# A two-block layer kernel on one core: the first W2 turned by VectorE instead of TensorE, and the attention constants made two row groups later

## The reference

```python
xn = _layernorm(x)
s = _L0_attn_ref(xn, ...)                        # state starts at zero: xn + rmsnorm(xn @ M) for one matrix M
g = _silu(_L0_ffn_ref(xn, W1, W2, W3))
x = x + s * g
...
# a feed-forward part, the same in both blocks
hidden = jax.nn.silu(xn @ W1.T) * (xn @ W3.T)    # 1024 wide
hidden = fwht(hidden)                            # Walsh-Hadamard transform over the 1024
out = hidden @ W2.T
...
# attention of block 1 (causal, one head, 256 wide)
q, k, v = x_norm @ qkv[:, :K], x_norm @ qkv[:, K:2*K], x_norm @ qkv[:, 2*K:]
out = softmax(mask(q @ k.T / 16)) @ v @ o_proj + residual
```

## Time and profile before

| | |
|---|---|
| time, median of 3 runs | 355.83 us (355.63 to 355.95) |
| the profiled execution's own time | 355.57 us |
| its span on the core | 353.8 us |
| TensorE busy | 348.7 us, 99% |
| VectorE busy | 252.5 us, 71% |
| ScalarE busy | 168.3 us, 48% |
| GpSimd busy | 106.3 us, 30% |

### The profile page before, as it was taken

One profiled execution on the slowest core, in us unless ns is written; L12 is line 12 of the kernel. 1 busy time (PEld: TensorE's weight loads), 2 busy tenths in 40 slices (PEclk: granted clock), 3 DMA queues, 4 the chain that ended last, 5 costly groups with the idle time before them and its releaser, 6 DMA issues.

```text
span 353.8 us, 4943 instructions
## 1 busy us (share of the span) xinstructions
PE 348.7 (99%) x1761; PEld 295.9 (84%) x1761; DVE 252.5 (71%) x498; ACT 168.3 (48%) x332; POOL 106.3 (30%) x122
## 2 busy tenths in 40 slices
PE   8999999999999999999999999999999999999996
PEld 5888888888888888888978878888888888888896
DVE  5679964995499666966588876788657886467645
ACT  2865442447254713454465644654346544464510
POOL 2164410466126943663025030150300703004000
PEclk9999999999999999999999999999999999999999
DMA  7989769205160403130342401626014251054001
GB/s 239 255 184 225 150 111 130 74 26 138 41 143 13 120 0 119 31 122 0 104 138 51 127 2 59 179 45 196 3 56 144 70 159 50 1 191 134 3 0 61
DMA packets 69648, 34.44 MB, mean 97 GB/s; under 512 B 40692, under 2 KB 69624, under 8 KB 69624
## 3 DMA queue, kind: packets, MB, share of 16 engines
q1 hardware_dynamic: 69480, 34.06, 38.0%
q10 hardware_dynamic: 144, 0.07, 0.1%
HBM read 21.99 MB, written 12.12 MB: 96 GB/s over the span
## 4 chain that ended last, share of the span: by engine, by line
PE 94%; ACT 2%; DVE 2%; DMA 1%; SPq 0%; issue 0%; ACTq 0%
PE GU L358 20%; PE GU L359 20%; PE GU L360 20%; PE O L358 8%; PE O L359 8%; PE O L360 8%; DMA stage<-in_L_ffn_W 1%; PE O L426 1%; PE O L509 1%; PE O L508 1%; PE O L507 1%; PE T L365 1%; PE T L360 1%; PE T L358 1%; PE T L359 1%; ACT PZ L809 1%
## 5 line engine op out<-in xcount | busy, mean ns | idle before, releaser
L722 ACT ACTIVATE hf<-GU 128x512 f32<-128x512 f32 x64 | 38.2, 599 | 80.4 <-DVE hid L841 64.3
L997 DVE TENSOR_TENSOR hf<-hf,GU 128x512 f32<-128x512 f32 x64 | 43.5, 680 | 28.4 <-PE GU L360 22.6
L358 PE MATMUL GU<-XT,W1T 128*128 128x512 f32 x128 | 50.6, 396 | 0.1
L841 DVE TENSOR_TENSOR hid<-hf,hid 128x512 fp32r<-128x512 f32 x64 | 50.5, 791 | 0.3
L360 PE MATMUL GU<-XT,W1T 128*128 128x512 f32 x128 | 49.9, 390 | 0.0
L359 PE MATMUL GU<-XT,W1T 128*128 128x512 f32 x128 | 49.9, 390 | 0.0
L358 PE MATMUL GU<-XT,W3T 128*128 128x512 f32 x128 | 49.9, 389 | 0.0
L360 PE MATMUL GU<-XT,W3T 128*128 128x512 f32 x128 | 49.8, 389 | 0.0
L359 PE MATMUL GU<-XT,W3T 128*128 128x512 f32 x128 | 49.8, 389 | 0.0
L358 PE MATMUL O<-hid,W2hi 128*128 128x512 f32 x112 | 44.0, 393 | 0.0
L359 PE MATMUL O<-hid,W2hi 128*128 128x512 f32 x112 | 43.7, 390 | 0.0
(11 more groups left out here) (204 smaller groups left out, 724.9 us busy)
## 6 DMA issues: line engine op xcount, KB each, us to landing
swap_rows<-GX SPq DMA_DIRECT2D x7, 512.0 KB, 3.3
sT<-swap_rows SPq DMA_DIRECT2D x28, 128.0 KB, 2.7
swap_gate<-GX SPq DMA_DIRECT2D x7, 512.0 KB, 2.9
sT<-swap_gate SPq DMA_DIRECT2D x28, 128.0 KB, 2.7
stage<-in_L_ffn_W SPq DMA_DIRECT2D x12, 256.0 KB, 4.3
swap_p<-PX SPq DMA_DIRECT2D x4, 640.0 KB, 3.4
PL<-swap_p SPq DMA_DIRECT2D x16, 160.0 KB, 3.1
stage<-in_L_ffn_W SPq DMA_DIRECT2D x32, 64.0 KB, 2.7
```

The source lines that it names most:

```text
L358: pe.matmul(o, lhs(0), rhs(0), start=start, stop=False)
L722: act.activation(hf[:, c % 2, :], GU[:, c % 2, 0, :], ACT.Silu).then_inc(silu_done, 1)
L841: dve.tensor_tensor(dst, src, hi_part.bitcast(F32), ALU.subtract).then_inc(done, 1)
L997: dve.tensor_tensor(hf[:, c % 2, :], hf[:, c % 2, :], GU[:, c % 2, 1, :], ALU.mult).then_inc(mul_done, 1)
```

## The change

1. Block 0's W2 is fetched by `load_blocks` straight into `U2[0]`, turned there by VectorE (`turn_w2(0, j)`), rounded by ScalarE (`turned_nat_hi`), and its residue is made by GpSimd (`nat_lo`). TensorE's transposes of W2, and the two splits that read their bank, are gone. W1 and W3 pairs of block 0 go round six staging parts (`load_first`).
2. TensorE's head is in another order: the four Hadamard steps stand behind chunks 3, 4, 5 and 6 (before: 0, 1, 3 and 5), pair 3 is transposed behind chunk 4 (before: 3), and `small_m` stands directly behind the last Hadamard step and the small transpose.
3. The attention constants are made in groups 1 and 2: `turn_wqkv` in group 1 behind chunk 5, four roundings on ScalarE behind chunk 6, four residues on GpSimd (`av_residues`), the products as three-part ones (24 matmuls of 256 columns instead of 8 float32 ones) behind chunk 0 of group 2, AR's and VR's parts behind chunk 2 of group 2. That group's first Hadamard step moves from behind chunk 1 to behind chunk 3, and waits for those parts (`sm_lo` 3).
4. The second group's statistics, normalisation and turn come earlier in VectorE's head; the transfers that carry its rows stand before those of qkv and the later x.
5. One quad step of block 0's butterflies moves from GpSimd to VectorE (`last_quad`).

```diff
+            def load_first(i):
+                for w, m in enumerate((W1[0], W3[0])):
+                    if i == PAIRS - 1:
+                        sp.wait_ge(w_tr, w + 1)
+                    sp.dma_start(first_part(i, w).rearrange("p (a k) -> p a k", a=2),
...
+            load_first(2)
             sp.dma_start(X[:, TILES:2 * TILES, :], xt_dram[:, TILES:2 * TILES, :]).then_inc(xnext_loaded, 16)
-            sp.wait_ge(w2_tr, 1)
-            load_pair(0, 2, stage[:, 0, :, :], stage_loaded[0])
+            load_blocks(U2[0][:, :, :].rearrange("p c d -> p (c d)"), W2[0], w2_loaded[0])
...
+            move_rows(1)
+            sp.dma_start(X[:, 2 * TILES:, :], xt_dram[:, 2 * TILES:, :]).then_inc(xrest_loaded, 16)
             load_blocks(wqkvT[:, :, :, :].rearrange("p w c d -> p (w c d)"), qkv, wqkv_loaded)
...
             def small_av():
+                pe.wait_ge(av_lo, 4)
+                pe.wait_ge(u_ready, PAIRS + 1)
...
+                for q, (left, right) in enumerate(((part(0), part(1)), (part(2), part(3)))):
+                    for i in range(KC):
+                        for c in range(KC):
+                            last = mm3(T[:, q, i * D:(i + 1) * D], lambda a: left(a, c)[:, i * P:(i + 1) * P], lambda a: right(a, c), c == 0, c == KC - 1)
+                    last.then_inc(sm_mm, 1)
...
                 head_pair(1)
                 first_up_chunk()
-                head_hadamard(0)
-                head_pair_w2(1)
                 up_chunk(0, 0, 1, True)
-                head_hadamard(1)
                 head_pair(2)
-                head_pair_w2(2)
                 up_chunk(0, 0, 2, True)
                 up_chunk(0, 0, 3, True)
+                head_hadamard(0)
+                up_chunk(0, 0, 4, True)
+                head_hadamard(1)
+                head_pair(3)
+                up_chunk(0, 0, 5, True)
                 head_hadamard(2)
...
+                up_chunk(0, 0, 6, True)
                 head_hadamard(3)
                 small_natural()
-                up_chunk(0, 0, 6, True)
                 small_m()
                 up_chunk(0, 0, 7, True)
-                small_av()
                 pe.wait_ge(sm_lo, 1)
                 recurrent_mix(0)
...
                     up_chunk(0, n, c, False)
-                    if c == 1 and n > 1:
+                    if c == 0 and n == 2:
+                        small_av()
+                    if c == (3 if n == 2 else 1) and n > 1:
+                        if n == 2:
+                            pe.wait_ge(sm_lo, 3)
                         next_hadamard(PAIRS + 2 * n - 3)
...
+            def last_quad():
+                dve.wait_ge(fly, 10)
+                a, b = ([V[:, HC // 2 + 2 * e:HC // 2 + 2 * e + 2, :].rearrange("p a d -> p (a d)") for e in (0, 1)] for V in (U2[0], U[0]))
+                dve.tensor_tensor(b[0], a[0], a[1], ALU.add).then_inc(fly_quad, 1)
+                dve.tensor_tensor(b[1], a[0], a[1], ALU.subtract).then_inc(fly_quad, 1)
...
+                if c == 5 and n == 1:
+                    turn_wqkv()
+                if c == 2 and n == 2:
+                    small_lo(1)
+                    small_lo(2)
```

More of the change, by code:

```diff
@@ L70, in two_block_kernel @@
         MR = sb("MR", [P, 2, KC, D], F32R)
+        with ExitStack() as early:
+            wqkvT = sb("wqkvT", [P, 3, KC, D], F32, early)
+            wo = sb("wo", [P, KC, D], F32, early)
         AR = sb("AR", [P, 2, KC, D], F32R)
@@ L175, in two_block_kernel @@
         ident_loaded, hadm_loaded, mask_loaded = sem("ident_loaded"), sem("hadm_loaded"), sem("mask_loaded")
+        first_loaded = [[sem(f"first{i}_loaded{w}") for w in (0, 1)] for i in range(PAIRS)]
         stage_loaded = [[sem(f"stage{i}_loaded{w}") for w in range(3)] for i in (0, 1)]
@@ L228, in _ @@
             out_dram = out.rearrange("b (t p) d -> p (b t) d", p=P)
[L230 to L237, removed]
+            def load_first(i):
[3 more added lines that the diff above has]
+                    sp.dma_start(first_part(i, w).rearrange("p (a k) -> p a k", a=2),
+                                 m[bass.ds(2 * P * i, 2 * P), :].rearrange("(a p) k -> p a k", p=P)).then_inc(first_loaded[i][w], 16)
             def load_blocks(to, src, done):
@@ L407, in head_hadamard @@
                     pe.wait_ge(hadm_ready, 1)
-                if i >= 1:
+                else:
                     pe.wait_ge(u_ready, i)
-                pair_hadamard(i, w2nat)
+                pe.wait_ge(natx_ready, i + 1)
+                pe.matmul(O[:, 1, :], hadmR[:, :], w2nat[:, 0, :, :].rearrange("p a d -> p (a d)"), start=True, stop=False)
+                pe.matmul(O[:, 1, :], hadmR[:, :], w2nat[:, 1, :, :].rearrange("p a d -> p (a d)"), start=False, stop=True).then_inc(h_done, 1)
             def small_natural():
                 pe.wait_ge(small_loaded, 16 * N_SMALL)
-                pe.wait_ge(w2nat_ready, PAIRS)
                 pe.transpose(O[:, 0, 0:2 * KC], gbrow[:, :], ident[0:2 * KC, 0:2 * KC]).then_inc(gb_tr, 1)
@@ L775, in block0_group @@
                     chunk(n, c, False)
-                    if c == 2 and n > 1:
+                    if c == 6 and n == 1:
+                        for w in range(3):
+                            hi(avH[:, 2 * w + 1, :, :], wqkvT[:, w, :, :], wqkv_turned, w + 1, av_hi)
+                        hi(avH[:, 7, :, :], wo[:, :, :], wo_loaded, 16, av_hi)
+                    if c == 2 and n == 2:
+                        small_hi([(R[:, 0, :, :].rearrange("p k d -> p (k d)"), T[:, q, :]) for q, R in enumerate((AR, VR))], 2, sm_mm, 2, sm_hi)
+                    if c == (4 if n == 2 else 2) and n > 1:
                         pair_u(1, PAIRS + 2 * n - 3, 2 * n - 3)
@@ L1306, in block0_group @@
                 else:
-                    last_butterfly(1, 25)
+                    last_butterfly(1, 23)
             def block1_group(n, x_at, last=False):
```

213 lines of the change are left out of this document (95 added, 118 removed).

## The result

| | before | changed |
|---|---|---|
| median | 355.80 us (6 runs, 355.56 to 355.96) | 362.08 us (6 runs, 361.73 to 365.17) |
| ratio | | 1.0187, interval 1.0170 to 1.0205 |
| profiled execution, span | 355.57, 353.8 | 362.27, 360.5 |
| TensorE busy | 348.7 | 349.5 |

The change makes the kernel slower by 6.3 us, where 3.5 were forecast. TensorE's busy time is no guide here: its list lost 16 transposes, and a stretch at a slow clock filled it up again.

The account below looks back on a forecast made before the run. TensorE's list was taken to bound the kernel. Head 0.15, group 2's attention products 3.0 and its late residue 0.35 summed to 3.5 us more: 359.3 us, own range 357.8 to 361, whole range 355.9 to 362.0.

Parts of the forecast that it names:

- the first stand: Head, before the first Hadamard step: TensorE waits about 2.2 us for W2's residue, made through VectorE, ScalarE and GpSimd.
- gb: Head, before `small_m`: TensorE waits 1.1 us for ScalarE's rounding of gamma and beta or `pair_u`, their cover being gone.
- MR: Head, before the recurrent mix: TensorE waits 0.9 us for M's residue on VectorE, behind the quad and sums.
- hid: Head, before the third down chunk: TensorE waits 0.45 us for VectorE's last residue, behind chunk 7's product.
- w2nat: Group 2's Hadamard step: TensorE waits 0.35 us for GpSimd's residue, pushed back by AR's and VR's residues on VectorE.
- It starts that down chunk at about 50.05: End of the head: TensorE starts the third down chunk at about 50.05 us, against 49.9 before.
- the transfers at 0: SyncE's queue: block 1's W2 is issued late, about when the first gate can be moved; cost taken as 0.
- with 3 us to spare: Head: W2 in 128-byte pieces lands at 18.4 us, against 21.4 when VectorE wants it, so hidden.
- The clock was a rival: Mid-kernel stands drop TensorE's clock to 1.2 GHz; two slow chunks give 364.7 us; within 0.12 for clock, contention or transfers.
- `last_butterfly` 2.73: 44.2: End of the head: GpSimd's last butterfly of W2 takes 2.73 us and ends at 44.2 us.
- The high bound: GpSimd's chain: three contention meetings with VectorE add 1.6 us, giving 360.9 us.
- Group 1's 0: Group 1: the moved qkv turns delay VectorE by 1.9 us, costing up to 0.3 at the down chunks; taken as 0.

Follow-up runs that it names:

- run 3: The kernel before with only the attention constants moved to groups 1 and 2 (part 3 of the change): 356.35 us, ratio 1.0015.
- run 9: The changed kernel with eight transfers of block 1's second W1 and W3 pair issued behind the gate's move on SyncE: 361.13 us, ratio 1.0140.
- run 5: The changed kernel with eight dummy products in TensorE's first stand and pair 3's residues ahead of the k vector on VectorE: 363.13 us, ratio 1.0211.
- run 10: The changed kernel with the edits of run 5 and run 9 together: 360.52 us, ratio 1.0127.
- run 1: The changed kernel with eight dummy products in TensorE's stand before the first Hadamard step: 362.39 us, ratio 1.0189.
- run 8: The changed kernel with pair 3's butterfly moved from GpSimd to VectorE as well: 363.18 us, ratio 1.0224.
- run 2: The changed kernel with VectorE's first W2 turn ahead of chunk 2's product and the statistics, and GpSimd's residue ahead of its rstd: 363.89 us, ratio 1.0224.
- run 12: Run 11's kernel without the eight dummy products: 359.76 us, ratio 1.0099.
- run 11: Run 10's kernel with pair 3's butterfly and W2's last butterfly on VectorE too: 359.24 us, ratio 1.0090.
- run 6: The changed kernel with the last quad butterfly back on GpSimd (part 5 undone): 364.13 us, ratio 1.0246.
- run 7: The changed kernel with the qkv turns moved from behind chunk 5 to the start of group 1 on VectorE: 362.77 us, ratio 1.0194.

## Why the prediction was wrong in size

**Right.** The direction; what bounds the kernel; the first stand (2.2 forecast, 2.17 measured), with its place, 24.15 against 24.43, and its chain of three engines. The stands for gb (1.1, measured 0.81), MR (0.9, measured 0.51) and hid (0.45, measured 0.17) came somewhat small; TensorE itself came to them some 2 us later than forecast (to the mix at 44.9 instead of 42.8), so that they are of the right order is partly luck. Group 2 was forecast at 3.0 for the products and 0.35 for w2nat; it costs 3.1. The products take 2.87 (100.38 to 103.25), the rest is spread over small delays at the changes between operands. The 0.35 didn't come: GpSimd's residue ended at 122.74 for a step at 123.00. That the new products cost more in group 2 (3.18) than leaves the head (2.29) is what run 3 shows by itself: 0.57 us slower.

Two readings of the prediction are loose, and nothing hangs on them: the one wait of before is for VectorE's `hf` and not for data to arrive, and its own range starts at 357.8 where the low bound is 358.2.

**Where the miss lies.** Most of it is in the head. "It starts that down chunk at about 50.05": the third down chunk started at 52.70. The lateness can be followed in the profile: the first step came 0.28 late, the second 1.94 (29.29 for 27.35), GpSimd's last residue ended 1.9 late (36.52 for 34.6), and the last butterfly 2.8 late (47.00 for 44.2). Two terms of the sum failed there, the clock at nothing and the butterflies at their undisturbed length. A third failed in group 1, the transfers at 0.

**The transfers: "SyncE issues block 1's W2 late, about when the first gate is ready to be moved; I take 0."** I had costed the blocks up to their own landing, and not by what they do to the transfers behind them. Four transfers of W2 in blocks held SyncE 8.66 us, every later transfer moved back with them, and the gate's scatter went out behind 17 us of issuing blocks, some of which were still being moved. Run 9 prices it at 0.95 us in the changed kernel. Behind a shorter head it costs more, 2.6 us between runs 5 and 10, because it is a floor: in runs 1, 5 and 8 it took back what the head gained. The landing of W2, forecast for 18.4 "with 3 us to spare", was at 20.4 in run 2; VectorE came for it at 21.57 in the changed kernel, so if it lands there at the same time some 1.2 us were to spare and this cost nothing. The Trainium skill, DMA: Bandwidth & Descriptors, section Specifications, says that transfers need pieces of 512 bytes or more for line rate. The trace agrees: with mostly 128-byte pieces the core moved 84 to 150 GB/s from 12 to 20 us, against 314.

**The clock was a rival and should have been a term.** The sum has it at nothing; it fell in three of the changed kernel's six runs. In the profile it added 1.7 us to one chunk and step, not the two chunks that the rival priced at 364.7. In time it is worth 0.4 us there (362.25 against 361.84, without the one of 365.17, which was not profiled), 0.7 in run 9 (361.47 and 361.54 at 0.995, 360.75 and 360.80 at 1.0 and 0.998), and 1.3 in run 12. The more of the other lists is cleared away, the more of it shows. As I read it, TensorE's lateness first covers that of VectorE and of the transfers. One such cover stands in the rows: the prediction had no term for pair 3's residues on VectorE, which stand behind the k vector. In the changed kernel they ended at 33.98 and TensorE, itself late, took them up at 34.03; at full clock it stood 1.67 us for them (run 1). That the stand of 2.2 us brings the clock down is shown by where it fell in the profiles; with the dummy products it was at 0.998 or more in 18 of 21 executions (runs 1, 5, 10 and 11), and why it was at 0.994 in the other three, of 365.6 to 366.6 us, is open.

**The last butterfly.** "`last_butterfly` 2.73: 44.2" was 3.42 and ended at 47.00. It starts 2.1 late, since the slow chunk and the first stand's 0.3 moved the four steps and one quad operation took 1.72, and it is 0.7 longer beside VectorE's sums. W2lo's stand of 1.05 follows. With this butterfly and pair 3's on VectorE, run 11 gains 1.28. The high bound had put 1.6 on three such meetings in GpSimd's chain, so their size was within reach, but I took the low end. I had cited the Trainium skill, GPSIMD Engine Reference, section Specifications, for contention between instructions of GpSimd and VectorE's with two SBUF inputs; it names those in a 2-port mode as well. The trace agrees on two inputs: in run 1 an operation of 0.22 us took 1.33. The normalisation, with one tensor input, was held up too, 2.29 us for four at 22.79 beside GpSimd and 1.38 without; in which mode it ran no run here shows.

**Group 1's 0.** It became 0.7, of which 0.6 lies before the mix (61.00 to 83.81, 22.8 us, where before took 22.2) and 0.1 between the mix and group 1's first down chunk. The 0.6 needed the late gate: with the gate on time it is gone, turns and all (runs 3 and 9).

The ladder of runs 9, 10, 11 gives back 0.95, 0.6 and 1.28, 2.8 us in all, which is the amount by which the forecast was short. That is not a proof that its other terms were each right, since run 11 also removes the forecast stands at MR. What is left in run 11 is 3.3 us over before by the medians and 3.8 by the spans of the profiles, of which 3.2 lie in group 2, 0.5 before group 1's first up chunk and 0.1 behind its mix. No version was found that beats before. Why the executions of runs 5 to 8 differ by 2 to 5 us, while those of runs 10 and 11 agree within 0.3, was not traced; in the first the gate's scatter goes out among blocks, in the second it doesn't.

## What to carry over

Price a transfer twice: by the time it takes to land, and by how far it pushes back the transfers behind it. Here small pieces cost the second more than the first (8.66 us of issuing for four transfers instead of 0.47 each), and the bill came 50 us later, at a small transfer that VectorE waited for and that then shared the way with late blocks.

When several engines' lists are equally full, taking away one engine's wait shows the next engine's. A stand is then worth what the next floor leaves of it, so an experiment that removes one wait and gains nothing doesn't clear that wait; repeat it with the floor lifted.

If a kernel has no idle TensorE in its middle, every new stand of about 2 us may bring a slow clock as well, and that belongs in the sum.

## What the hardware showed that I had not expected

- The same stand of 2.2 us was followed by the lower clock in some executions and not in others of one kernel: three of six in the changed kernel, two of six in run 12. Where it fell, the step and half a chunk behind it ran slow, 1.7 us longer in all, and then it was back to full.
- Issuing 1 MB as 32x32 blocks held SyncE between 5.46 and 8.66 us, by its place in the list (5.46 and 8.66 are in the two queues shown; 7.08 in run 9). What sets it was not traced.
- A scatter of one transfer took 2.9 us from its issue to the gather's with nothing in front of it, 4.4 to 5.6 behind blocks; its own issue went from 0.39 to 1.87 us.
- A VectorE operation on 64 columns (0.22 us) was held up to 1.33 us beside one GpSimd operation, about that one's whole length (1.30), and two more up to 0.78 us beside butterflies of 0.74. Here contention is priced by GpSimd's instruction, not by VectorE's own.
